# One attention and feed-forward block on one core: q and k as two float32r parts in 64-row tiles, in place of three bf16 parts, and a new order of the work

## The chip, the core and the metric

The kernel runs on one core of a Trainium2 chip. The metric is the device time of one execution in microseconds (us). TensorE (PE) does the matrix products, VectorE (DVE), ScalarE (ACT) and GpSimd (POOL) the elementwise work, and SyncE (SP) issues every DMA.

## The reference, cut to what matters

```python
def stablemax3(logits):                      # in place of a softmax
    logits = logits - max(logits, axis=-1)
    pos = 1.0 + x * (1.0 + 0.5 * x * (1.0 + x / 3.0))
    neg = 1.0 / (1.0 - x * (1.0 - 0.5 * x * (1.0 - x / 3.0)))
    s = where(x >= 0, pos, neg); return s / sum(s)
# x is (8, 512, 128); 16 heads of 8 dimensions
sa, ca, ga, sb, cb, gb = (silu(c) @ wmod)    # ga, gb: sign(g) * max(|g|, 0.25)
h = layernorm(x) * (1 + ca) + sa
q, k, v = h @ w_qkv.T                        # per head (512, 8)
o = stablemax3(q @ k.T * 8 ** -0.5) @ v
x = x + ga * (o @ w_out.T + b_out)
h = layernorm(x) * (1 + cb) + sb
f = relu(s0 * ([h, -h] @ K0)) * 2            # K: +1 or -1; widths 512, 512, 128
x = x + gb * (s2 * (relu(s1 * (f @ K1)) * 2 @ K2))
```

After the maximum is taken off, x is never above 0, so only `neg` counts: one over a cubic. The kernel writes that cubic with its root ROOT = -0.596 split off, and takes 1/|.| with a reciprocal square root of a square.

## The kernel before

Eight batches are worked through one after another, each in 16 steps `n`. A step handles 512x512 logits of one head, twice. First with queries on the partitions (`logits`, L486, PSUM tile SA), from which DVE takes each query's maximum (`maxima`, L749). Four heads (a quad) later the 16 columns of maxima are turned by PE (L496), negated by DVE (L761), split in three bf16 parts by POOL (L941 to L949) and brought by DMA (L1072) into rows 96 to 98 of QH, against rows of ones in KH. Second with keys on the partitions (`scores`, L465, PSUM tile Z, two halves `h`): now the matmul takes the maximum off as it goes. ACT squares a half with a shift (L557, `sq`), DVE makes the cubic from it and Z (L737, `cub`), POOL squares the cubic in place (L890; three heads of 16, letter A in ON_POOL, on ACT instead, L567), ACT takes the reciprocal root (L582, `prob`), and PE multiplies with V and a column of ones (`with_v`, L510, tile OP, four heads in four column tiles of 32).

q and k are needed at more precision than one bf16 has. Each is split in three bf16 parts (POOL, L922 to L932), written to DRAM and read back with each part three times, so that 72 rows of one matmul hold all nine products of parts (PARTS = 3, NROW = 72).

Each engine's instructions stand in one fixed order, written out by hand. Besides its head, a step carries a piece of the work of other batches, called misc: the layernorm, q, k and v of the next batch, the output projection x1 of the last one, and the feed-forward layers l0, l1, y of the one before that (`MISC` gives the step and the place, 0 or 1, of each product, `EVENTS` those of the small work). A step on PE is

```python
logits(n, (0, 1)); with_v(n); scores(b, n + 1, 0); misc_at(pe, b, n, 0)
logits(n, (2,)); maxima_across(n); logits(n, (3,)); misc_at(pe, b, n, 1); scores(b, n + 1, 1)
```

on DVE cubic, maxima, misc, cubic, maxima, misc, and on ACT square, relu, square, prob of two heads back (BEHIND = 2), relu. Waits that tie them: a half of Z is free when DVE has read it (`z_taken`, s_cv); a bank of SA when its maxima are taken (s_mx); one of F_RING = 3 buffers of `cub` when its `prob` is made (s_p); the DMAs of a quad's maxima must have landed before its scores (s_mrow). MB is one PSUM bank for all misc products. The loop is unrolled.

Of the kernel before, what the change touches and what calls it, by code (L numbers as in the profile page):

```python
# [7 lines left out]
BF16 = mybir.dt.bfloat16  # L8
# [18 lines left out]
PARTS = 3  # L27
NROW = PARTS * PARTS * HD
MROW = 96

EPS = 1e-5
TWO_ONES = float(np.array([0x3F803F80], np.uint32).view(np.float32)[0])
E_DMAS = PARTS + 1
SCALE = HD ** -0.5
FIRST = -1

F_RING = 3
P_RING = 8
# [24 lines left out]
def short(name, off, step, place=0, point="e"):  # L69
    return name, off, [(step, place, CHUNKS)], (step, point)  # L70


def long_(name, off, step):

    return name, off, [(step, 0, CHUNKS // 2), (step, 1, CHUNKS // 2)], (step + 1, "s")


MISC = [
    short("hT", 1, 0), short("q", 1, 1), short("k", 1, 2), short("h2T", -2, 3),
    short("l0_0", -2, 4), short("l0_1", -2, 5), short("l0_2", -2, 6), short("l0_3", -2, 7), short("v", 1, 8),  # L80
    long_("l1_0", -2, 9), long_("l1_1", -2, 10), long_("l1_2", -2, 11), short("x1", -1, 12), long_("l1_3", -2, 13),
    ("y", -2, [(14, 0, 2), (14, 1, 1), (15, 0, 1)], (15, "e")),
]
# [11 lines left out]
EVENTS = {
    "den_sq": (7, 1), "den_inv": (8, 0), "att": (8, 1, "pool"), "st2": (13, 0), "mv2": (14, 0), "rs2": (14, 1),  # L100
    "x1n": (15, 0, "pool"), "w2g": (11, 1), "wog": (5, 1), "xbg": (7, 1),
}
# [8 lines left out]
def is_first(b):
    return isinstance(b, int) and b == FIRST


def misc_of(b):
    return MISC_LAST.get(b, MISC) if isinstance(b, int) else MISC


def event(b, name):
    return EVENTS_LAST.get(b, {}).get(name, EVENTS[name]) if isinstance(b, int) else EVENTS[name]  # L120


def live(beta):

    return not isinstance(beta, int) or 0 <= beta < B


def adaln_block(nc, x, w_qkv, w_out, b_out, k0, k1, k2, s0, s1, s2, c, wmod, out):
    x_t = x.rearrange("b (t p) d -> p (b t) d", p=P)

    parts_q = nc.dram_tensor("parts_q", (NQ, PARTS, QUAD * HD, S), BF16, kind="Internal").ap()
    parts_k = nc.dram_tensor("parts_k", (NQ, PARTS, QUAD * HD, S), BF16, kind="Internal").ap()
# [3 lines left out]
    with ExitStack() as ctx:  # L136
# [80 lines left out]
        k2u = k_u8[:, 4096:4096 + KC * D].rearrange("p (a n) -> p a n", a=KC)  # L217

# [5 lines left out]
        s_apart = sem("s_apart")  # L224
# [19 lines left out]
        s_w2g = sem("s_w2g")  # L244
        s_parts = {n: sem("s_parts_" + n) for n in "qk"}
# [4 lines left out]
        s_fa = sem("s_fa")  # L250
# [44 lines left out]
        def apart(eng, b):


            if not isinstance(b, int):
                eng.sem_inc(s_apart)

        def z_taken(eng, b, n, h):

            need(eng, s_cv, 2 * H * b + 2 * n + h + 1)

        def quad_before(b, n):

            return (b, n // QUAD + 1) if n // QUAD < NQ - 1 else (b + 1, 0)


        tail = [(b, i) for b in (B - 1, B, B + 1) for i, m in enumerate(misc_of(b))  # L310
                if b > B - 1 or m[2][0][0] > 8]
# [11 lines left out]
        def products_at(b, n, points):

            return [(name, b + off, bank_of(b, i)[0]) for i, (name, off, _, (step, point)) in enumerate(misc_of(b))
                    if step == n and point in points and live(b + off)]

        def logits_bank(b, beta, h, qt):

            pair = (TB * h + qt) // 2  # L330
            if is_first(b) and pair % 3:
                return Z[:, pair % 3 - 1, :].rearrange("p (t s) -> p t s", t=2)
            return SA

        def batches(body):

            def run(eng):
                for b in range(FIRST, B + 2):
                    body(b)
            return run  # L340
# [775 lines left out]
```

## Time and profile before

| | |
|---|---|
| device time, median of 3 runs | 837.32 us (834.61 to 837.56) |
| profiled execution, its own time | 835.29 us |
| its span, first to last instruction | 833.5 us |
| mean granted clock of TensorE | 0.948 of full speed |
| busy PE / DVE / ACT / POOL | 78% / 80% / 74% / 71% of the span |

1.8 us of the profiled execution lie outside the span. A busy share counts the union of an engine's instructions; four engines between 71% and 80% mean that they work in turns somewhere, and only stretches of the trace tell where.

### The profile page before, as it was taken

What the parts mean: (1) busy time and instruction counts of PE and PEld (TensorE: products, weight loads), DVE (VectorE), ACT (ScalarE), POOL (GpSimd) and SP (SyncE); (2) the same over time, 40 slices, a digit from 0 to 9 for tenths busy, and PEclk for the clock granted to TensorE, in tenths of its full rate; (3) what the DMA queues carried; (4) which work ended last, traced back from release to release, by engine and by line L of the source; (5) the groups of instructions that cost most, each with busy time, mean ns of one, the idle gap of its engine ahead of it and who ended that gap; (6) DMA issues with size and microseconds to landing.
All of it is one profiled execution on the core that took longest, in us unless ns stands there. A gap on an engine that the chain in (4) does not pass through costs nothing.

```text
span 833.5 us, 9550 instructions
## 1 busy us (share of the span) xinstructions
PE 648.3 (78%) x2897; PEld 224.3 (27%) x2897; DVE 664.4 (80%) x785; ACT 620.6 (74%) x541; POOL 595.3 (71%) x507
## 2 busy tenths in 40 slices
PE   3076777777777898779977898679877997996887
PEld 2022111111121333223422342123421342341244
DVE  5389899989997889887998889798997889866120
ACT  1005789889888888698788788698779789889621
POOL 7306887789887967977887967977798677775310
PEclk9968599989999999999999999999999999997999
DMA  2211111210221002210131012210221012000100
GB/s 79 71 60 55 49 38 54 71 56 24 71 65 52 28 28 84 76 41 0 59 94 56 20 39 84 69 37 7 63 80 60 6 42 71 7 8 6 44 22 13
DMA packets 34996, 39.39 MB, mean 47 GB/s; under 512 B 6376, under 2 KB 28160, under 8 KB 34944
## 3 DMA queue, kind: packets, MB, share of 16 engines
q1 hardware_dynamic: 34944, 38.77, 14.7%
q8 instruction: 24, 0.39, 0.2%
q14 instruction: 28, 0.23, 0.1%
HBM read 25.77 MB, written 8.40 MB: 41 GB/s over the span
## 4 chain that ended last, share of the span: by engine, by line
PE 37%; DVE 22%; issue 15%; POOL 14%; ACT 10%; DMA 2%; DVEq 0%; ACTq 0%; SPq 0%; POOLq 0%
PE MB L435 11%; DVE mx L749 10%; DVE cub L737 8%; POOL cub L890 7%; PE Z L465 6%; PE OP L510 5%; PE SA L486 5%; ACT sq L557 4%; ACT prob L582 2%; PE SA L435 2%; POOL rem L925 2%; PE MB L444 2%; PE MB L428 2%; POOL SQ L932 1%; ACT cub L567 1%
## 5 line engine op out<-in xcount | busy, mean ns | idle before, releaser
L890 POOL TENSOR_TENSOR cub<-cub 128x2048 f32<-128x2048 f32 x104 | 373.8, 3597 | 66.5 <-DVE cub L737 66.5
L737 DVE SCALAR_TENSOR_TENSOR cub<-sq,Z 128x1024 f32<-128x1024 f32 x256 | 309.4, 1210 | 48.5 <-ACT sq L557 48.3
L749 DVE TENSOR_REDUCE mx<-SA 128x2 f32<-128x1024 f32 (+1 forms) x277 | 303.1, 1098 | 53.4 <-PE SA L486 51.7
L557 ACT ACTIVATE sq<-Z,shift 128x1024 f32<-128x1024 f32 x256 | 281.3, 1114 | 69.8 <-PE Z L465 68.9
L582 ACT ACTIVATE prob<-cub 128x2048 f32<-128x2048 f32 x128 | 244.7, 1912 | 35.9 <-POOL cub L890 35.9
L486 PE MATMUL SA<-KH,QH 96*128 96x512 bf16 x492 | 165.9, 400 | 89.8 <-DVE mx L749 42.8
L465 PE MATMUL Z<-QH,KH 128*128 128x512 bf16 x512 | 162.5, 400 | 68.0 <-DVE cub L737 66.0
L510 PE MATMUL OP<-prob,Vq 128*16 128x512 f32 x1024 | 140.1, 622 | 3.1 <-ACT OT L612 3.1
L435 PE MATMUL MB<-hid,W 128*128 128x512 f32 x216 | 101.2, 593 | 0.9 <-ACT hid L600 0.9
L486 PEld LDWEIGHTS SA<-KH,QH 96*128 96x128 bf16 x492 | 42.0, 100 | 216.5 <-issue 108.2
L465 PEld LDWEIGHTS Z<-QH,KH 128*128 128x128 bf16 x512 | 35.7, 99 | 234.7 <-DVE cub L737 161.6
L600 ACT ACTIVATE hid<-MB,sv 128x512 f32<-128x512 f32 x54 | 37.0, 686 | 52.3 <-PE MB L435 43.3
L941 POOL TENSOR_SCALAR mp<-ms 16x128 bf16<-16x128 f32 x32 | 9.2, 288 | 80.0 <-DVE ms L761 80.0
L435 PEld LDWEIGHTS MB<-hid,W 128*128 128x128 f32 x216 | 40.6, 189 | 37.6 <-issue 30.7
L567 ACT ACTIVATE cub<-cub 128x2048 f32<-128x2048 f32 x24 | 45.8, 1909 | 0.0
L428 PE MATMUL MB<-h2T,W 128*128 128x512 f32 x54 | 32.9, 696 | 0.0
L510 PEld LDWEIGHTS OP<-prob,Vq 128*16 128x16 f32 x1024 | 17.4, 95 | 56.6 <-issue 53.5
L860 POOL TENSOR_TENSOR rs<-mv,eps 128x4 f32<-128x4 f32 x16 | 3.2, 197 | 31.1 <-DVE mv L790 26.1
L444 PEld LDWEIGHTS MB<-W2G,hid 128*128 128x128 f32 x192 | 23.9, 192 | 2.2
L444 PE MATMUL MB<-W2G,hid 128*128 128x128 f32 x192 | 24.0, 275 | 0.0
L612 ACT ACTIVATE OT<-OP 128x512 f32<-128x512 f32 x32 | 18.9, 591 | 5.4 <-PE OP L510 5.4
L833 DVE TENSOR_TENSOR y<-SA,x1k 128x512 f32<-128x512 f32 x2 | 1.4, 690 | 26.2 <-PE SA L444 26.2
(125 smaller groups left out, 508.6 us busy)
## 6 DMA issues: line engine op xcount, KB each, us to landing
QH<-parts_q SPq DMA_DIRECT2D x96, 96.0 KB
KH<-parts_k SPq DMA_DIRECT2D x32, 288.0 KB
nd<-OT SPq DMA_DIRECT2D x128, 32.0 KB
parts_q<-SQ SPq DMA_DIRECT2D x24, 128.0 KB
parts_k<-SK SPq DMA_DIRECT2D x24, 128.0 KB
xa<-L_attn_x SPq DMA_DIRECT2D x8, 256.0 KB, 8.7
xb<-L_attn_x SPq DMA_DIRECT2D x8, 256.0 KB, 8.9
out<-y SPq DMA_DIRECT2D x8, 256.0 KB, 2.2
```

Of the source, the lines that this page charges most:

```text
L428: mm = nc.tensor.matmul(bank, W0[:, m * P:(m + 1) * P], h2T[:, :], start=True, stop=True)
L435: mm = nc.tensor.matmul(bank, W1[:, kc, m * P:(m + 1) * P], hid[0][:, kc, :], start=(kc == 0), stop=(kc == KC - 1))
L444: mm = nc.tensor.matmul(bank4[:, t, :], hid[1][:, kc, t * P:(t + 1) * P], W2G[:, kc, :], start=(kc == 0), stop=(kc == KC - 1))
L465: mm = nc.tensor.matmul(Z[:, h, t * S:(t + 1) * S], KH[:, n, k0_:k0_ + P], QH[:, n, :], start=True, stop=True)
L486: nc.tensor.matmul(logits_bank(b, beta, hh, qt)[:, qt % 2, :], QH[0:MROW, hh, qt * P:(qt + 1) * P], KH[0:MROW, hh, :], start=True, stop=Tr ...
L510: mm = nc.tensor.matmul(OP[32 * j:32 * j + 2 * HD, :], Vq[:, tb, hh, :, :].rearrange("p d a -> p (d a)"), prob[:, hh % P_RING, tb * S:(tb ...
L557: nc.scalar.activation(sq[:, h, :], Z[:, h, :], ACT.Square, bias=shift[:, 0:1]).then_inc(s_sq, 1)
L567: nc.scalar.activation(f, f, ACT.Square).then_inc(s_fa, 1)
L582: nc.scalar.activation(prob[:, m % P_RING, :], cub[:, (H * beta + m) % F_RING].rearrange("p a n -> p (a n)"), RSQRT).then_inc(s_p, 1)
L737: nc.vector.scalar_tensor_tensor(cub[:, (H * b + n) % F_RING, h, :], sq[:, h, :], CUB_ADD, Z[:, h, :], ALU.add, ALU.mult).then_inc(s_cv, 1)
L749: nc.vector.tensor_reduce(mx[:, g % 2, j * TB + qts[0]:j * TB + qts[-1] + 1], logits_bank(b, beta, QUAD * g + j, qts[0])[:, qts[0] % 2:qts ...
L890: nc.gpsimd.tensor_tensor(ff, ff, ff, ALU.mult).then_inc(s_fp, 1)
```

## The change

q and k are split in two float32r parts (a 4-byte type whose writer rounds away the low bits of the mantissa): the first part is the rounded copy that ACT writes, the second is the rest, made by DVE in one pass. All four products of parts take 32 rows. Row 32 is a product of 0 and 1, rows 33 and 34 hold the two parts of the maximum, 35 and 36 the constant. So scores contract 37 rows and logits 33, and two heads stand beside each other at rows 0 and 64 (`e`), each matmul in a row tile of 64 with an output bank of its own. A step (`m`, `group`) is no longer one head: it is two heads by half of the keys for scores, two heads by two blocks of queries for logits. Each unit of DVE and ACT stays 128x1024.

The maxima are split by DVE (L679, L681) in place of POOL; all 128 squares of the cubic are on POOL; `cub` and `prob` have 4 buffers; `prob` stands one step behind in place of two (BEHIND = 1); the products with V end at the 8th step after the quad's first in place of the 10th; the maxima run 6 steps ahead of the scores (AHEAD = 6). Misc products stand at three places of a step (a, c, d), mostly one matmul each. The large memsets of QH and KH are gone; small constants are written and brought in by DMA.

```diff
-PARTS = 3
+PARTS = 2
-ON_POOL = "PPPPPAPPPPAPPPPA"
-BEHIND = 2
+RING = 4
+AHEAD = 6
+BEHIND = 1
+AV_BEHIND = 4
-    long_("l1_0", -2, 9), long_("l1_1", -2, 10), long_("l1_2", -2, 11), short("x1", -1, 12), long_("l1_3", -2, 13),
+    ("l1_0", -2, [(3, "a", 1), (3, "c", 1), (3, "d", 1), (4, "a", 1)]),
+    ("x1", -1, [(8, "a", 4)]),
...
-        QH = sb("QH", [P, H, S], BF16)
+        QH = sb("QH", [P, 2 * NQ, S], F32R)
...
+                for e in range(2):
+                    rows = slice(64 * e, 64 * e + K_Z)
+                    mm = nc.tensor.matmul(Z[:, h, e * S:(e + 1) * S], KH[rows, 2 * g + r, keys], QH[rows, 2 * g + r, :],
+                                          start=True, stop=True)
+                mm.then_inc(s_z, 1)
...
+            m = s + AHEAD
+            scores(s + 1, 0)
+            if m % QUAD == 0 and m >= QUAD:
+                logits(m, 0, (1,))
+            misc("a")
+            logits(m, 1, (0, 1))
+            with_v(s)
+            scores(s + 1, 1)
+            misc("c")
+            maxima_across(m)
+            logits(m + 1, 0, (0,) if (m + 1) % QUAD == 0 and m + 1 >= QUAD else (0, 1))
+            misc("d")
...
+            square_of(s + 1, 0)
+            take("a")
+            square_of(s + 1, 1)
+            take("c")
+            take_numerators(s)
+            prob_of(s - BEHIND)
+            take("d")
...
-                nc.vector.tensor_scalar(ms[:, :], SA[0:QUAD * TB, 1, 0:P], -1.0, MAX_SHIFT, ALU.mult, ALU.add)\
+                nc.vector.tensor_copy(mp[:, i, 0, :], SA[0:QUAD * TB, 1, 0:P]).then_inc(s_mh, 1)
+                dve.wait_ge(s_mh, quad + 1)
+                nc.vector.tensor_tensor(mp[:, i, 1, :], SA[0:QUAD * TB, 1, 0:P], mp[:, i, 0, :].bitcast(F32), ALU.subtract)\
+                    .then_inc(s_mp, 1)
...
+            cubic(s, 0)
+            take_maxima(m)
+                maxima(m, 0, (0, 1))
+            split(b, n)
+            cubic(s, 1)
+            maxima(m, 1, (0, 1))
+            take(b, n, "a")
+            misc()
...
-            nc.gpsimd.memset(QH[:, :, :].bitcast(F32), 0.0).then_inc(s_one, 1)
-            nc.gpsimd.memset(KH[:, :, :].bitcast(F32), 0.0).then_inc(s_one, 1)
-                        nc.gpsimd.tensor_tensor(dst[:, 2, :], rem[:, i, :], dst[:, 1, :], ALU.subtract)\
...
+            if (s + AHEAD - 4) % QUAD == 0 and 0 <= s + AHEAD - 4 < GROUPS:
+                sp.wait_ge(s_mp, quad + 1)
+                for e in range(2):
+                    for a in range(PARTS):
+                        r = 64 * e + R_MAX + a
+                        sp.dma_start(QH[r:r + 1, 2 * g:2 * g + 2, :].bitcast(F32), mp[2 * TB * e:2 * TB * (e + 1), quad % 2, a, :].bitcast(F32))\
+                            .then_inc(s_mrow[g], 16)
```

What stands on PE where the second layer of the feed-forward (l1, `MB<-hid,W`) runs, before (SA is logits, Z scores, OP the products with V; L435 is l1):

```order
L486 MATMUL SA<-KH,QH 128x512 x2
L510 MATMUL OP<-prob,Vq 16x512 x4
L465 MATMUL Z<-QH,KH 128x512 x2
L435 MATMUL MB<-hid,W 128x512 x2
L486 MATMUL SA<-KH,QH 128x512 x2
L435 MATMUL MB<-hid,W 128x512 x2
L465 MATMUL Z<-QH,KH 128x512 x2
```

and in the changed program (L446 logits, L427 scores, L467 V, L387 l1):

```order
L427 MATMUL Z<-QH,KH 128x512 x2
L387 MATMUL MB<-hid,W 128x512
L446 MATMUL SA<-KH,QH 128x512 x2
L467 MATMUL OP<-prob,Vq 16x512 x4
L427 MATMUL Z<-QH,KH 128x512 x2
L387 MATMUL MB<-hid,W 128x512
L446 MATMUL SA<-KH,QH 128x512 x2
L387 MATMUL MB<-hid,W 128x512
```

Two l1 products in a row stood ahead of logits or scores; now one does, and the scores' first half stands ahead of all else in the step.

On POOL at the split of q and k of the next batch, before (cub is the square of the cubic, SQ and SK the parts of q and k, rem the rest):

```order
L890 TENSOR_TENSOR cub<-cub 128x2048
L922 TENSOR_SCALAR SQ<-rem 128x512
L925 TENSOR_TENSOR rem<-rem,SQ 128x512
L929 TENSOR_SCALAR SQ<-rem 128x512
L932 TENSOR_TENSOR SQ<-rem,SQ 128x512
L890 TENSOR_TENSOR cub<-cub 128x2048
L922 TENSOR_SCALAR SK<-rem 128x512
```

and in the changed program, from the same steps to the two layernorms (L774, L776 roots, L814 xn and x1n):

```order
L808 TENSOR_TENSOR cub<-cub 128x2048 x4
L824 COPY Vq<-Vn 128x4x32
L837 TENSOR_TENSOR woG<-wo,gA 128x128
L808 TENSOR_TENSOR cub<-cub 128x2048
...
L814 TENSOR_SCALAR xn<-xa,mv,rs 128x128 x4
L808 TENSOR_TENSOR cub<-cub 128x2048
L774 TENSOR_TENSOR rs<-mv,eps 128x4
L776 TENSOR_TENSOR rs<-rs,half 128x4
L814 TENSOR_SCALAR x1n<-x,mv,rs 128x128 x4
```

The eight passes on q and k have left POOL; both layernorms now follow each other with one square between them.

On DVE at the maxima of a quad, before (L761 negates them, L749 reduces):

```order
L737 SCALAR_TENSOR_TENSOR cub<-sq,Z 128x1024
L761 TENSOR_SCALAR ms<-SA 16x128
L749 TENSOR_REDUCE mx<-SA 128x1 x2
L737 SCALAR_TENSOR_TENSOR cub<-sq,Z 128x1024
```

and in the changed program (L657 cubic, L679 and L681 the two parts, L690 the second part of k):

```order
L657 SCALAR_TENSOR_TENSOR cub<-sq,Z 128x1024
L679 CAST mp<-SA 16x128
L681 TENSOR_TENSOR mp<-SA,mp 16x128
L668 TENSOR_REDUCE mx<-SA 128x1 x2
L690 SCALAR_TENSOR_TENSOR SK<-MB,SK 128x512
L657 SCALAR_TENSOR_TENSOR cub<-sq,Z 128x1024
```

One small pass of DVE per quad is added, and POOL no longer stands between DVE and the DMA.

## Rows read from the trace of the kernel before

**Rows 1.** The page: the span, and each engine's busy time and instructions

```profile
span 833.5 us, 9550 instructions
PE 648.3 (78%) x2897; PEld 224.3 (27%) x2897; DVE 664.4 (80%) x785; ACT 620.6 (74%) x541; POOL 595.3 (71%) x507
```

**Rows 2.** Windows: stretch, length, busy PE, PEld, DVE, ACT, POOL, clock, DMA

```profile
61.60:150.50 88.90, 64.58 (x256) 15.10 (x256) 83.93 (x91) 70.14 (x57) 65.06 (x49) 0.85 0.17 54
...
239.40:328.20 88.80, 74.10 (x353) 26.87 (x352) 76.76 (x91) 73.41 (x65) 71.75 (x64) 0.98 0.14 44
```

**Rows 3.** The same windows for line L737, the cubic: DVE busy, count

```profile
61.60:150.50 88.90, 41.07 (x34) 0.85 0.17 54
...
239.40:328.20 88.80, 37.52 (x31) 0.98 0.14 44
```

**Rows 4.** Groups by line and shape: busy, mean ns, idle before and its releaser

```profile
L890 POOL TENSOR_TENSOR cub<-cub 128x2048 f32<-128x2048 f32 x104 | 373.8, 3597 | 66.5 <-DVE cub L737 66.5
L737 DVE SCALAR_TENSOR_TENSOR cub<-sq,Z 128x1024 f32<-128x1024 f32 x256 | 309.4, 1210 | 48.5 <-ACT sq L557 48.3
...
L749 DVE TENSOR_REDUCE mx<-SA 128x2 f32<-128x1024 f32 x215 | 262.1, 1219 | 53.0 <-PE SA L486 51.3 <-issue 1.1
...
L435 PE MATMUL MB<-hid,W 128*128 128x512 f32 x216 | 101.2, 593 | 0.9 <-ACT hid L600 0.9
L567 ACT ACTIVATE cub<-cub 128x2048 f32<-128x2048 f32 x24 | 45.8, 1909 | 0.0
...
L761 DVE TENSOR_SCALAR ms<-SA 16x128 f32<-16x128 f32 x32 | 8.8, 274 | 3.0 <-PE SA L496 2.7
```

**Rows 5.** Timeline of DVE in the third batch: start, us, idle before

```profile
338.31 1.21 DVE L749 TENSOR_REDUCE mx<-SA 128x2 f32<-128x1024 f32 x1
339.45 1.21 DVE L737 SCALAR_TENSOR_TENSOR cub<-sq,Z 128x1024 f32<-128x1024 f32 x1
...
343.00 1.22 DVE L737 SCALAR_TENSOR_TENSOR cub<-sq,Z 128x1024 f32<-128x1024 f32 x1 [1.21 <-ACT sq L557]
```

**Rows 6.** Timeline of PE around one product with V

```profile
310.78 0.60 PE L486 MATMUL SA<-KH,QH 96*128 96x512 bf16 x2
...
311.30 1.05 PE L510 MATMUL OP<-prob,Vq 128*16 128x512 f32 x8
...
312.29 0.60 PE L465 MATMUL Z<-QH,KH 128*128 128x512 bf16 x2
...
312.73 1.95 PE L444 MATMUL MB<-W2G,hid 128*128 128x128 f32 x16
```

**Rows 7.** Timeline of POOL: first and last of four passes on q, and on maxima

```profile
239.66 0.62 POOL L922 TENSOR_SCALAR SQ<-rem 128x512 bf16<-128x512 f32 x1 [1.82 <-DVE rem L816]
...
242.31 1.16 POOL L932 TENSOR_TENSOR SQ<-rem,SQ 128x512 bf16<-128x512 f32 x1
...
258.11 0.29 POOL L941 TENSOR_SCALAR mp<-ms 16x128 bf16<-16x128 f32 x1
...
259.36 0.42 POOL L949 TENSOR_TENSOR mp<-mrem,mp 16x128 bf16<-16x128 f32 x1
```

**Rows 8.** Timeline: the first layernorm, first logits, first scores, last cubics, a last layernorm

```profile
6.37 7.17 DVE L681 TENSOR_SCALAR xn<-xa,mv,rs 128x128 f32<-128x128 f32 x4
...
41.41 1.01 PE L486 MATMUL SA<-KH,QH 96*128 96x512 bf16 x2 [19.06 <-DMA KH<-parts_k]
...
61.59 1.01 PE L465 MATMUL Z<-QH,KH 128*128 128x512 bf16 x2 [1.32 <-DVE mx L749]
...
774.30 2.35 DVE L737 SCALAR_TENSOR_TENSOR cub<-sq,Z 128x1024 f32<-128x1024 f32 x2 [3.01 <-ACT sq L557]
...
802.43 1.11 DVE L799 TENSOR_SCALAR x1n<-x,mv,rs 128x128 f32<-128x128 f32 x4 [1.41 <-POOL rs L862]
```

**Rows 9.** Line L1072, the DMAs of the maxima: issue ns, and landing

```profile
L1072 SPq DMA_DIRECT2D QH<-mp x96: 524/585/3390, 56.9 to 742.0; - x96
DMA to landing us min/median/max: 1.7/2.2/7.4
```

More of the change, by code:

```diff
@@ L111, in is_first @@
[L111 to L120, printed above, removed]
-def live(beta):
-    return not isinstance(beta, int) or 0 <= beta < B
+MAIN = [
[10 rows of a table added]
+]
+MISC = {b: MAIN for b in range(FIRST, B - 1)}
+MISC[B - 1] = [
[9 rows of a table added]
+]
+MISC[B] = [
[6 rows of a table added]
+]
+MISC[B + 1] = [
+    ("l1_2", -2, [(0, "a", 2), (0, "c", 2)]), ("l1_3", -2, [(1, "a", 2), (1, "c", 2)]),
+    ("y", -2, [(2, "a", 4)]),
+]
@@ new lines, with group @@
+BY_DVE = ("x1", "v", "y")
+MAIN_AT = {"xbg": 6, "wog": 5, "den_sq": 6, "den_inv": 7, "att": 7, "st2": 9, "mv2": 10, "rs2": 11, "x1n": 11,
+           "w2g": 8, "st1": 6, "mv1": 7, "rs1": 9, "xn": 10}
+AT = {b: MAIN_AT for b in range(FIRST, B)}
+AT[B - 1] = MAIN_AT | {"w2g": 4, "st2": 8, "mv2": 9, "rs2": 9, "x1n": 9}
+AT[B] = MAIN_AT | {"w2g": 2, "st2": 8, "mv2": 8, "rs2": 9, "x1n": 9}
+AT[B + 1] = MAIN_AT | {"w2g": 0}
+TAIL = ("att", "x1n")
+def live(beta):
+    return 0 <= beta < B
+def group(m):
+    i = m % QUAD
+    return m // H, m % H // QUAD, i % 2, i // 2 * 2
@@ L290, in need @@
         def need(eng, s, n):
-            if not isinstance(n, int) or n > 0:
+            if n > 0:
                 eng.wait_ge(s, n)
[L295 to L311, printed above, removed]
@@ L323, in products_at @@
[L323 to L340, printed above, removed]
@@ L345, in adaln_block, with unit_bank, unit_before, steps @@
+        def unit_bank(m, u):
+            k = 2 * m + u
+            return Z[:, k % 3 - 1, :].rearrange("p (e s) -> p e s", e=2) if k < 8 and k % 3 else SA
+        def unit_before(m, u):
+            k = 2 * m + u
+            return 2 * (k - 2) if k < 8 else 2 * k
+        def steps(body):
+            for s in range(FIRST * H, (B + 2) * H):
+                body(s)
+        def at(s, name, beta_off, b, n):
+            return AT[b][name] == n and live(b + beta_off)
         block = ctx.enter_context(nc.Block())
@@ new lines, in logits @@
+                if heads[0] == 0:
+                    if m == 0 and u == 0:
+                        pe.wait_ge(s_gate, 1)
+                        pe.wait_ge(s_rows, 4 * 16)
+                    if m % QUAD == 0 and u == 0:
+                        pe.wait_ge(s_qk[g], (beta + 1) * LOADS * 16)
+                    need(pe, s_mx, unit_before(m, u))
+                else:
+                    need(pe, s_mp, m // QUAD)
+                for e in heads:
+                    rows = slice(64 * e, 64 * e + K_LOG)
+                    nc.tensor.matmul(unit_bank(m, u)[:, e, :], QH[rows, 2 * g + r, qt * P:(qt + 1) * P],
+                                     KH[rows, 2 * g + r, :], start=True, stop=True).then_inc(s_a, 1)
@@ L995, in pool_batch @@
-            for n in range(H):
-                misc(n, 0)
-                square_of(n)
-                misc(n, 1)
+            if n == 0 and live(b - 2):
+                pool.wait_ge(s_taken["x1"], b - 1)
+                need(pool, s_taken["y"], b - 2)
+                nc.gpsimd.tensor_scalar(x1k[:, :, :], x1[:, :, :], 1.0, 0.0, ALU.mult, ALU.add).then_inc(s_x1k, 1)
+            if n in (1, 5):
+                v_in(b, 2 if n == 1 else 3)
+            if n in (13, 14):
+                v_in(b + 1, n - 13)
```

840 lines of the change are left out of this document (340 added, 500 removed), and 23 rows, old and new, of tables (MAIN, MISC).

## The prediction

> **What bounds the kernel now.** I read the page first. Four engines are busy 71% to 80% of 833.5 us [rows 1], so none bounds the whole, and the stretches decide. The windows, cut at 88.9 us from the first scores on, show two regimes. In the first one, before any feed-forward work has begun, DVE is busy 83.93 of 88.90 us, 94%: the kernel runs at DVE's pace. In the third, with l0, l1 and y on PE, DVE is busy 76.76 of 88.80, 86%, and no other engine is fuller [rows 2]. The same windows for the cubic turn that into steps, since each step has two cubics: 34 of them in 88.90 us are 5.23 us a step, 31 in 88.80 are 5.73 [rows 3]. DVE's own work is 76.76 / 15.5 = 4.95 us a step, the rest is waiting. The groups say for what: the cubic waited 48.5 us in all for ACT's squares, the maxima 53.0 for PE's logits, and POOL's squares 66.5 for DVE [rows 4]. Where DVE is fed, a 128x1024 pass starts every 1.14 us (338.31 to 339.45); at 343.00 it stood 1.21 us for ACT [rows 5]. That comes after POOL has spent about 3.8 us on q (239.66 to 243.47) and as much on k between two squares [rows 7]: POOL late, ACT's prob late, ACT's next square late. So the reader is to see a kernel near DVE's limit, with some 12 us of waiting in each of the batches that carry feed-forward work.
>
> **The change, part by part.**
>
> *DVE.* Cubics and maxima stay 512 passes of 128x1024. q and k keep one pass each. Added are one small pass per quad, like the 0.274 us of L761 [rows 4], and a wait of it on the one before, which I put at 0.1: 0.37 x 4 / 16 = 0.09 a step. DVE's work becomes 4.95 + 0.09 = 5.04 us a step.
>
> *POOL.* It loses the passes on q and k, 3.8 us each of which 3.6 are work, 16 times, and on the maxima 1.7 us (258.11 to 259.78), 1.4 of it work, 32 times [rows 7]: 57 + 45. It gains 24 squares. All 128 at 3.597 are 460; the other work was 595.3 - 373.8 = 221.5 [rows 1, 4], less 102, less about 8 of memsets. Sum 571, or 71 us a batch of 16 steps: under DVE's 81, by little. From n = 5 to 11 seven squares (25.2) meet both layernorms, w2g, att, xbg and the roots, which I add up to 14 us: 39 against 37 in which DVE does its seven steps. With four cub buffers a square may be late by roughly a step before ACT is held, so I charge little.
>
> *ACT.* It loses 24 squares of 1.909, 5.7 us a batch [rows 4], and gains two copies of q and k. It has room.
>
> *PE.* Eight matmuls of 512 columns a step, 0.44 for two (312.29 to 312.73) [rows 6], 1.76 in all. The trace has no float32r and no row tile. Bounds for a pair of heads: below, one bf16 matmul, 0.22; above, two l1 products, each two passes of 101.2 / 216 = 0.47 [rows 4], 1.9. I take 0.22 to 0.25. For the single pass speaks that the operand carries fewer bits than the f32 of l1, which pays two recorded passes. For side by side speaks the product with V: four f32 matmuls of 512 columns, in four column tiles, take 0.99 (311.30 to 312.29), where four l1 products one after another take 3.8 [rows 4, 6]. So PE saves about 0.85 a step, 14 us a batch. Against that stand switches between tilings, since every misc product now lies between row tiles. The column-tiled product starts 0.52 after the logits ahead of it where 0.44 would be due [rows 6]; I call it 0.1 a switch, and 29 misc pieces a batch, two switches each, make 6 us. PE: 74.10 a window, 76 a batch, less 14, plus 6 = 68 of 84. The Trainium skill (TensorEngine Tiling (Array Packing), Key Properties) says that a change of tiling mode, not just of tile, drains TensorE; the 0.08 above agrees in kind. By the rule with this price PE has 68, without it 62, and the forecast is 790 by either, as PE is last in neither; only at 0.4 a switch, 23 us, would it be.
>
> *Order.* Say DVE's step begins at 0 with cubic 0. Cubic 0 ends at 1.15, maxima 0 at 2.3, cubic 1 at 3.45, maxima 1 at 4.6. PE makes scores 0 at 1.2, one l1 product until 2.5, logits by 2.9 (due 3.45), V until 4.0, scores 1 by 4.4, one product until 5.4, logits by 5.8 (due 6.2). Each misc place holds one product of 0.94 and fits. Before, two stood together ahead of logits or scores. So I give the batches with feed-forward work the share of DVE that the first had, 95%: 5.04 / 0.95 = 5.3 a step.
>
> *Maxima.* They are made two passes into DVE's step, at 1.85, four DMAs later (3 x 0.585 + 2.2 for the last) they have landed at 5.8; the scores want them at 5.3 + 1.2 = 6.5 [rows 9]. Hidden by 0.7 us. If the landing is 7.4, the longest of before, PE stands 4.5 us, and queued behind it are the logits that DVE needs. At n = 6 SP issues the six loads of the next batch's first quad, which wait for all parts of q and k (1 MB in place of 0.77), ahead of a quad's maxima. I charge 4 us in the run for this and POOL together.
>
> *Start.* The first layernorm took 7.17 us on DVE while POOL wrote QH and KH; the same four passes took 1.11 at 802.43 [rows 8]. That is up to 6 us, I take 5. The parts leave sooner, with more bytes, and I let these cancel but for 1: first logits at 41.4 - 5 + 1 = 37.5. From there to the first scores were 20.2 us. Now four steps' maxima (8 x 1.14), turning and splitting (about 1.5) and the DMA (4) make 15: first scores at 53, against 61.6.
>
> *End.* From the end of the last cubic (774.30 + 2.35 = 776.65) to 833.5 are 56.9 us, nearly all the second half of the last batch's feed-forward work on PE, as before. I take 57.
>
> **The sum.** Before: 61.6 + 715 + 56.9 = 833.5. After: 53, then 112 steps x 5.3 = 594, 80 for the last batch (10 steps at 5.3, 6 without maxima at 4.5, bound by ACT and POOL) and 4 for the waits, then 57: 788, and 1.8 outside the span: 790 against 835.3 profiled. The runs' median is 837.3, 0.25% higher, which I leave within the range.
>
> **The rivals.**
>
> *Row tiles run one after another* (15%). A pair costs 0.44, PE is at 68 + 14 = 82 us a batch, as full as DVE, and logits behind a misc product come 0.3 late. Five batches with feed-forward work at 5.6 a step: 790 + 24 = 814.
>
> *The maxima's DMA or POOL's clump is last* (15%). Once a batch the maxima land 2 to 4 us late, behind loads, or x1n's four passes hold a square by over a step. 8 x 3 = 24: 814.
>
> *DVE is fed throughout* (10%). 98% in place of 95%: 5.14 a step, 18 us less: 771. Against it speaks that even without feed-forward work before had 94%.
>
> *A float32r matmul is no single pass* (9%): the slower side. PE without these matmuls is 68 - 14 = 54 us a batch; with p for a pair, 54 + 64 p. Eight such batches and the 110 us of start and end pass today's 833 at p = 0.57; at p = 0.7 they give 900, and at 0.94, an l1 product's price with the two heads side by side, 1020. I name 900.
>
> *Nothing is gained* (6%): PE, less busy, is granted 1.2 GHz for long. The first window had 0.85 of 2.4 GHz and still 5.23 a step [rows 2, 3]; at half speed all through PE would need 136 us a batch and so be full, which no row shows at that clock; at three quarters on average 68 / 0.75 = 91 a batch, as now: 835. The Trainium skill (TensorE: Matmul & The Clock Gate, HAM oscillation) holds that idle gaps make the clock fall; the 0.98 of the third window agrees as far as it goes, with PE busy there at 74.10.
>
> **How the numbers follow.** The forecast has 45%: 790, its own range 778 to 802. The range reaches down to 768 for DVE fed throughout and up to 822 for the two rivals at 814; outside are the last two and the tails of the others, 2 in 10. A measurement of this kernel can tell about 0.5% from no change. Faster: 45 + 10 + 15 + 15 = 85%. Within 0.5%: 4 of the last rival's 6. Slower: 9 + 2 = 11%.
>
> **What would show it.** Windows of the loop: 5.3 us a step in batches with and without feed-forward work, DVE at 95%. A pair's logits and scores start within 0.05 us of each other, and the next matmul 0.22 after. First scores at 53, xn under 3 us. PE waits for `QH<-mp` under 5 us in all, cubic for ACT under 20. No idle of ACT on POOL's squares beyond a few us, near n = 11. The forecast is wrong if pairs start 0.22 apart or more, if the maxima's DMAs stand in PE's waits with over 20 us, or if the clock in the middle windows is below 0.9 with PE on the chain.

## The result: 892.7 us against 836.7, the kernel is 6.7% slower

The changed kernel takes 892.7 us (median of 4 runs, 890.68 to 894.96) against 836.7 for the one before (834.61 to 837.56): a ratio of 1.067, 95% interval 1.064 to 1.071. The forecast was 790, its range 768 to 822.

The page of the changed kernel, profiled at a mean granted clock of 0.843 where before had 0.948:

```profile
span 888.7 us, 9519 instructions
PE 743.6 (84%) x2897; PEld 263.7 (30%) x2897; DVE 667.8 (75%) x814; ACT 591.1 (67%) x531; POOL 580.6 (65%) x350
```

As many matmuls as before take 743.6 us of PE in place of 648.3 [rows 1], where some 60 us fewer were forecast. DVE, POOL and ACT have the work that was worked out for them (POOL 571 forecast). The same 88.9 us windows as [rows 2, 3], the first from the first scores on, for all engines and then for the cubic, now L657:

```profile
58.40:147.30 88.90, 70.75 (x238) 23.65 (x238) 78.08 (x86) 60.70 (x51) 59.29 (x25) 0.97 0.13 43
239.40:328.20 88.80, 79.71 (x339) 28.34 (x337) 75.29 (x89) 68.35 (x62) 67.94 (x40) 0.88 0.16 49
...
58.40:147.30 88.90, 37.56 (x31) 0.97 0.13 43
239.40:328.20 88.80, 35.08 (x29) 0.88 0.16 49
```

31 and 29 cubics: 5.74 and 6.12 us a step, where before had 5.23 and 5.73 and the forecast 5.3. DVE is busy 88% and 85% of them, PE 90% of the second. The groups, in the columns of [rows 4]:

```profile
L668 DVE TENSOR_REDUCE mx<-SA 128x2 f32<-128x1024 f32 (+1 forms) x282 | 311.5, 1105 | 119.9 <-PE SA L446 117.3
L657 DVE SCALAR_TENSOR_TENSOR cub<-sq,Z 128x1024 f32<-128x1024 f32 x256 | 309.6, 1210 | 16.8 <-ACT sq L507 16.8
L518 ACT ACTIVATE prob<-cub 128x2048 f32<-128x2048 f32 x128 | 243.8, 1905 | 2.4 <-POOL cub L808 2.4
...
L387 PE MATMUL MB<-hid,W 128*128 128x512 f32 x216 | 128.2, 683 | 0.6 <-ACT hid L544 0.6
```

DVE's waits for ACT fell from 48.3 to 16.8 us and ACT waits 2.4 for POOL, as the change means it. The waits of the maxima for PE's logits rose from 51.7 to 117.3. And l1, whose matmuls the change doesn't touch, has a mean of 683 ns for 593 [rows 4].

Two views show why PE is late. First the clock. Windows of 600 us from the middle of the loop, first of the kernel before and then of the changed one, columns as in [rows 2]:

```profile
150.00:750.00 600.00, 493.99 (x2317) 171.32 (x2315) 523.10 (x598) 504.25 (x438) 481.49 (x407) 0.98 0.15 48
```

```profile
150.00:750.00 600.00, 538.07 (x2152) 183.56 (x2148) 500.41 (x585) 450.05 (x403) 439.49 (x252) 0.81 0.15 47
```

PE is busier and yet granted 0.81 in place of 0.98. The four f32 matmuls with V (one for each head of a quad, two recorded passes each) show it piece by piece: of the 128 such groups, 120 ran in 0.98 us and 5 at half speed (1.84) before, with 3 between; after, 70 and 44, with 14 between.

Second, what a step costs at full speed, by the lengths of its matmuls. The timeline of PE (y is L396, scores L427, logits L446, V L467; the last row is the first half of a piece), and a row of DVE in the same stretch:

```profile
411.02 1.16 PE L396 MATMUL MB<-W2G,hid 128*128 128x128 f32 x8
412.11 0.51 PE L446 MATMUL SA<-KH,QH 33*128 33x512 f32 x2
412.54 1.16 PE L396 MATMUL MB<-W2G,hid 128*128 128x128 f32 x8
413.63 0.50 PE L427 MATMUL Z<-QH,KH 37*128 37x512 f32 x2
414.06 1.16 PE L396 MATMUL MB<-W2G,hid 128*128 128x128 f32 x8
415.15 0.49 PE L446 MATMUL SA<-KH,QH 33*128 33x512 f32 x2
415.57 1.05 PE L467 MATMUL OP<-prob,Vq 128*16 128x512 f32 x8
416.56 0.50 PE L427 MATMUL Z<-QH,KH 37*128 37x512 f32 x2
416.99 0.71 PE L396 MATMUL MB<-W2G,hid 128*128 128x128 f32 x4
```

```profile
415.78 1.23 DVE L668 TENSOR_REDUCE mx<-SA 128x2 f32<-128x1024 f32 x1 [0.68 <-PE SA L446]
```

From start to next start PE has no gap: a misc piece 1.09, a pair 0.43, V 0.99. From 411.02 to 416.99 is one step, 5.97 us of PE alone against 5.04 of DVE's work: DVE stands 0.68 for logits. A pair was costed at 0.22 to 0.25, a misc piece at 0.94. Where no piece of another tiling follows, a pair takes 0.34.

The start and the end, in the same columns:

```profile
6.50 1.52 DVE L598 TENSOR_SCALAR xn<-xa,mv,rs 128x128 f32<-128x128 f32 x4
...
37.49 0.79 PE L446 MATMUL SA<-KH,QH 33*128 33x512 f32 x2 [20.66 <-DMA KH<-parts_k]
...
58.38 0.79 PE L427 MATMUL Z<-QH,KH 37*128 37x512 f32 x2 [4.11 <-DMA QH<-mp]
...
820.92 2.35 DVE L657 SCALAR_TENSOR_TENSOR cub<-sq,Z 128x1024 f32<-128x1024 f32 x2 [2.48 <-ACT sq L507]
```

So the span is 58.4, a loop of 764.9 to the end of the last cubic (823.3), and 65.4 behind it, against the forecast's 53, 678 and 57. In the chain of waits, PE has 59% of the span and the DMA of the maxima 4%.

### The profile page after: what moved, and what is told of

Its sections match the earlier page's. It is cut to its first block, busy times and chain, and to the rows that moved or that the text cites. A ratio compares the mean times of both kernels' runs of the same rounds, so it can differ in the third digit from the quotient of the medians.

```text
span 888.7 us, 9519 instructions
## 1 busy us (share of the span) xinstructions
PE 743.6 (84%) x2897; PEld 263.7 (30%) x2897; DVE 667.8 (75%) x814; ACT 591.1 (67%) x531; POOL 580.6 (65%) x350
## 4 chain that ended last, share of the span: by engine, by line
PE 59%; DVE 17%; issue 10%; DMA 6%; ACT 5%; SPq 2%; POOL 1%; DVEq 0%; ACTq 0%; POOLq 0%
PE MB L387 13%; PE OP L467 12%; PE SA L446 10%; PE Z L427 8%; DVE mx L668 7%; DVE cub L657 6%; DMA QH<-mp 4%; PE MB L396 3%; PE MB L380 3%; PE MB L361 3%; PE SA L387 2%; ACT prob L518 2%; SPq L948 2%; ACT sq L507 1%; DMA KH<-parts_k 1%
## 5 line engine op out<-in xcount | busy, mean ns | idle before, releaser
L808 POOL TENSOR_TENSOR cub<-cub 128x2048 f32<-128x2048 f32 x128 | 460.4, 3601 | 185.0 <-DVE cub L657 185.0
L668 DVE TENSOR_REDUCE mx<-SA 128x2 f32<-128x1024 f32 (+1 forms) x282 | 311.5, 1105 | 119.9 <-PE SA L446 117.3
L657 DVE SCALAR_TENSOR_TENSOR cub<-sq,Z 128x1024 f32<-128x1024 f32 x256 | 309.6, 1210 | 16.8 <-ACT sq L507 16.8
L446 PE MATMUL SA<-KH,QH 33*128 33x512 f32 x502 | 169.6, 600 | 64.9 <-DVE mx L668 44.1
L427 PE MATMUL Z<-QH,KH 37*128 37x512 f32 x512 | 157.4, 585 | 42.5 <-DVE cub L657 28.5
L467 PE MATMUL OP<-prob,Vq 128*16 128x512 f32 x1024 | 178.9, 780 | 0.0
L427 PEld LDWEIGHTS Z<-QH,KH 37*128 37x128 f32 x512 | 60.3, 223 | 237.3 <-issue 118.6
L387 PE MATMUL MB<-hid,W 128*128 128x512 f32 x216 | 128.2, 683 | 0.6 <-ACT hid L544 0.6
L446 PEld LDWEIGHTS SA<-KH,QH 33*128 33x128 f32 x502 | 64.8, 228 | 210.5 <-issue 103.1
L387 PEld LDWEIGHTS MB<-hid,W 128*128 128x128 f32 x216 | 34.3, 196 | 31.8 <-issue 29.6
L396 PE MATMUL MB<-W2G,hid 128*128 128x128 f32 x224 | 31.9, 287 | 0.9 <-ACT hid L544 0.9
L467 PEld LDWEIGHTS OP<-prob,Vq 128*16 128x16 f32 x1024 | 17.5, 99 | 46.2 <-issue 40.7
L774 POOL TENSOR_TENSOR rs<-mv,eps 128x4 f32<-128x4 f32 x16 | 3.3, 204 | 40.7 <-DVE mv L736 27.7
L396 PEld LDWEIGHTS MB<-W2G,hid 128*128 128x128 f32 x224 | 27.0, 191 | 8.4 <-issue 8.4
L824 POOL COPY Vq<-Vn 128x128 f32<-128x128 f32 x32 | 9.6, 301 | 25.0 <-DVE Vn L708 25.0
L814 POOL TENSOR_SCALAR x1n<-x,mv,rs 128x128 f32<-128x128 f32 x28 | 21.9, 794 | 0.7
L814 POOL TENSOR_SCALAR xn<-xa,mv,rs 128x128 f32<-128x128 f32 x28 | 21.9, 794 | 0.1
```

Source lines behind the costliest of these rows:

```text
L387: mm = nc.tensor.matmul(bank, W1[:, kc, m * P:(m + 1) * P], hid[0][:, kc, :], start=(kc == 0), stop=(kc == KC - 1))
L396: mm = nc.tensor.matmul(bank4[:, t, :], hid[1][:, kc, t * P:(t + 1) * P], W2G[:, kc, :], start=(kc == 0), stop=(kc == KC - 1))
L427: mm = nc.tensor.matmul(Z[:, h, e * S:(e + 1) * S], KH[rows, 2 * g + r, keys], QH[rows, 2 * g + r, :], start=True, stop=True)
L446: nc.tensor.matmul(unit_bank(m, u)[:, e, :], QH[rows, 2 * g + r, qt * P:(qt + 1) * P], KH[rows, 2 * g + r, :], start=True, stop=True).then ...
L467: mm = nc.tensor.matmul(OP[32 * j:32 * j + 2 * HD, :], Vq[:, tb, hh, :, :].rearrange("p d a -> p (d a)"), slot[:, tb % 2, j % 2, :], start ...
L657: nc.vector.scalar_tensor_tensor(cub[:, m % RING, h, :], sq[:, h, :], CUB_ADD, Z[:, h, :], ALU.add, ALU.mult).then_inc(s_cv, 1)
```

## The experiments

"From first to last cubic" below is the start of the first to the end of the last: 711.9 us before, 762.4 after. Ratios are to the kernel before, run on the same chip.

**What the tiles, the type and the rows cost.** Four kernels, each the changed one with other operands for scores and logits. `x_f32r_whole` contracts all 128 rows of both heads, so it has no row tiles; its sums mix two heads. `x_bf16_tiles` reads the upper half of each word as bf16, so that its products are less precise. `x_bf16_whole` does both. `x_f32r_rows64` keeps the tiles, and contracts all 64 rows of each, the added ones zeros (in logits also the rows of old maxima). Those with added rows write QH and KH full of zeros first.

```diff
-                    rows = slice(64 * e, 64 * e + K_Z)
+                    rows = slice(0, P)                # whole; rows64: slice(64 * e, 64 * e + 64)
...
-                    KH[rows, 2 * g + r, keys], QH[rows, 2 * g + r, :]
+                    KH[rows, 2 * g + r, keys].bitcast(BF16)[:, 1::2], QH[...].bitcast(BF16)[:, 1::2]   # bf16
...
+            nc.gpsimd.memset(QH[:, :, :].bitcast(F32), 0.0).then_inc(s_fill, 1)     # whole, rows64
+            nc.gpsimd.memset(KH[:, :, :].bitcast(F32), 0.0).then_inc(s_fill, 1)
```

> The changed kernel (892.7 us) with scores and logits contracted over all 128 rows, both heads' rows at once, still float32r; the logits and scores are wrong sums, and QH and KH are filled with zeros at the start. No row tiles are left, so no switch between row tiles and whole matmuls. Theory A (in the changed kernel the two row tiles do not save time over two whole matmuls, and the switches and the low clock that go with them are what it lost): a pair still holds PE 0.43 us, a misc product falls from about 1.0 back to 0.86, and V runs at full speed (1.05 us) in most steps; 845 to 865 us. Theory B (the tiles do work side by side, but one float32r matmul takes 0.43 us): a pair now holds 0.86, 4 x 0.43 us more in each step, 990 us or more. Theory C (the order of the work is what lost): within 1% of 892.

> The changed kernel with scores and logits reading the upper halves of the same float32r words as bf16, in the same row tiles; less precise q, k and maxima. Theory A: a pair still holds 0.43 us, 885 to 895 us, the clock as low. Theory B: a pair falls to 0.22, four pairs a step, 845 to 865 us. Theory C: within 1% of 892.

> Both edits: bf16 halves, contracted over all 128 rows, no row tiles; wrong sums. This is the matmul of the kernel before in the order of the changed one. Theory A: pair 0.43 us, clock as in the kernel before (0.95), 840 to 860 us; not far from x_f32r_whole. Theory B: the same time here, but 130 us under x_f32r_whole. Theory C: within 1% of 892.

> The changed kernel with both tiles contracting all their 64 rows (those above 37 are zero; logits now also contract stale rows of the maxima, so they are wrong). Time of a matmul and switches are the same. If the clock fell because few rows work, V runs at half speed in fewer of its 128 products and the time falls to 860 to 880 us; if rows don't matter, 892 within 1%.

Measured, with the clock of the profiled run. The last column is a step with three l1 products in which PE has no gap, from V to V at full speed:

| | time, us | ratio (95%) | clock | first to last cubic | first cubic at | step with three l1 |
|---|---|---|---|---|---|---|
| after | 892.7 | 1.067 (1.064 to 1.071) | 0.843 | 762.4 | 60.9 | 5.85 |
| x_f32r_rows64 | 865.35 | 1.034 (1.024 to 1.045) | 0.884 | 729.7 | 69.2 | 5.85 |
| x_bf16_tiles | 860.88 | 1.029 (1.018 to 1.040) | 0.849 | 731.1 | 60.6 | 5.48 |
| x_f32r_whole | 852.82 | 1.019 (1.009 to 1.030) | 0.957 | 716.1 | 70.1 | 5.60 |
| x_bf16_whole | 850.32 | 1.016 (1.005 to 1.028) | 0.930 | 714.7 | 69.7 | 5.47 |

The fill costs the kernels that have it some 9 us before the first cubic, so rows64 is 33 us faster than after where both do the same. It differs from after in the rows contracted and the fill alone: PE works on 27 and 31 more rows, nearly all zeros, each matmul takes as long as before (0.50 us recorded), and the clock rises. Its products with V are at full speed 98 times and at half 20, against 70 and 44. So the number of rows at work moves the clock, and giving the rows back returns 33 of the 50 us that the loop lost.

That is not yet a share of the loss. x_bf16_tiles has as few rows as after and a clock as low (46 products with V at half speed, 73 at full), and it gets 31 of the 50 us back as well, by its shorter steps. The rows with their clock, and the type, are each worth some 30 us while the other is as it is. All these kernels also work on other numbers than after; no run changes the numbers alone.

What a switch of tiling costs stands in the timelines, y at full speed between two pairs, of x_bf16_tiles and of x_f32r_whole:

```profile
404.33 0.40 PE L428 MATMUL Z<-QH,KH 37*128 37x512 bf16 x2
404.66 1.16 PE L397 MATMUL MB<-W2G,hid 128*128 128x128 f32 x8
405.75 0.40 PE L447 MATMUL SA<-KH,QH 33*128 33x512 bf16 x2
405.99 0.39 PE L428 MATMUL Z<-QH,KH 37*128 37x512 bf16 x2
```

```profile
403.63 0.73 PE L428 MATMUL Z<-QH,KH 128*128 128x512 f32 x2
404.20 1.05 PE L397 MATMUL MB<-W2G,hid 128*128 128x128 f32 x8
405.01 0.71 PE L447 MATMUL SA<-KH,QH 128*128 128x512 f32 x2
```

Two tiles do run side by side: with logits and scores behind each other, a bf16 pair takes 0.24 (405.75 to 405.99), as forecast, and 0.33 ahead of another tiling. With float32r it is 0.34 and 0.43. Its weight load is longer too, 0.18 for 0.095 us each; that this is the reason is likely, and no run shows it. Where the records part a pair from the piece behind it differs from kernel to kernel, so take the two together. From one l1 product over a pair to the next are 1.48 us in float32r tiles, 1.39 in bf16 tiles, 1.32 and 1.31 on the whole array; a pair and y have 1.52, 1.42, 1.38 and 1.36. So next to a piece the tiles cost some 0.15 us in float32r and 0.07 in bf16. Between two pairs they save 0.2 instead. By the last column, tiles in bf16 cost PE nothing in such a step and in float32r 0.25 us, and float32r costs 0.37 more than bf16 in tiles, 0.13 on the whole array. A float32r matmul is a single pass in every tiling.

**The maxima's DMA.** The waits for it that the trace gives PE and PE's weight loads add up to 33 us in after. Most of these stretches are in both lists; PE itself stood 13.1 us, 4.11 of them ahead of the first scores. Making the maxima a step earlier takes the waits off PE, if the rest stays.

```diff
-AHEAD = 6
+AHEAD = 7
```

> The changed kernel with the maxima, the loads of q and k and the DMAs of the maxima one step earlier (AHEAD 7 in place of 6), nothing else. PE waited 33 us for the DMAs of the maxima in the changed kernel. Theory D (these DMAs are on the path): the wait falls under 8 us and the time by 10 to 25 us, to 868 to 883. Theory A (they only fill time that PE's other delays make): the wait goes, the time stays within 5 us of 892.

> x_f32r_whole (852.8 us, wrong sums, no row tiles) with AHEAD 7. There PE waited some 50 us for the DMAs of the maxima. Theory D: 825 to 838 us, at or below the kernel before. Otherwise within 5 us of 852.

That the time falls was wrong in both. `x_ahead7`: 899.28 us, 1.076 (1.070 to 1.083), at the edge of what after has; PE stood 8.7 us in place of 13.1. `x_whole_ahead7`: 862.92, 1.034 (1.031 to 1.038), 10 us slower than x_f32r_whole; PE stood 29.6 us in place of 33.5. So neither run took the wait away, and neither shows what it costs. x_f32r_whole at one quad, from the timeline of SP, the chain of waits and the timeline of PE:

```profile
393.50 2.70 SPq L952 DMA_DIRECT2D QH<-mp  x4
...
395.57 5.00 DMA QH<-mp
...
400.62 0.74 PE L428 MATMUL Z<-QH,KH 128*128 128x512 f32 x2 [1.09 <-DMA QH<-mp]
```

and x_whole_ahead7 in the same place:

```profile
398.54 1.19 SPq L939 DMA_DIRECT2D KH<-parts_k  x2
399.84 2.70 SPq L952 DMA_DIRECT2D QH<-mp  x4
...
401.92 7.63 DMA QH<-mp
...
409.59 0.74 PE L428 MATMUL Z<-QH,KH 128*128 128x512 f32 x2 [0.99 <-DMA QH<-mp]
```

With AHEAD 7 SP issues the four DMAs directly behind the six loads of the next quad's q and k, 0.1 us after them in most quads, where with AHEAD 6 it was 2 us or more. From the issue of the last one to PE's scores they then take 7.2 to 9.1 us (the 20 times that they stand in the chain), against 3.0 to 6.9 with AHEAD 6. What the step gained was lost on the way; that the loads in front are the reason is not shown. Where no tiles slow PE down, the DMA is on the path: it has 11% of the chain of waits in x_f32r_whole and 12% in x_bf16_whole, where PE stands 41.1 us for it, against 4% in after; in the kernel before PE never waits for it.

**The rows alone.** The kernel before with fewer rows in its matmuls, nothing else changed. Both leave the maxima out of the scores; `b_rows37` also leaves out part of the products of q and k.

```diff
-    KH[:, n, k0_:k0_ + P], QH[:, n, :]
+    KH[0:72, n, k0_:k0_ + P], QH[0:72, n, :]          # b_rows37: 0:37
...
-    QH[0:MROW, hh, qt * P:(qt + 1) * P], KH[0:MROW, hh, :]
+    QH[0:72, hh, qt * P:(qt + 1) * P], KH[0:72, hh, :]
```

> The kernel before with scores and logits contracting the first 72 rows alone (no maximum is taken off in the scores, so the output is wrong); still whole-array bf16 matmuls, same durations and order. If the number of rows at work sets the clock, V runs at half speed in more than the 5 to 10 of 128 products of before, and the time rises by 5 to 25 us; if not, 835 within 1%.

> The same with 37 rows: few rows as in one tile of the changed kernel, and a row tile of 64, so with switches, but without two heads side by side; wrong output. By rows and switches: half speed in over 40 of 128 products with V, l1 products next to scores hold PE 0.2 us longer, 880 to 920 us. If neither rows nor switches cost, 835 within 1%.

`b_rows72`: 859.44 us, 1.030 (1.021 to 1.038), clock 0.861. 72 rows in place of 128 and 96, with instructions, order, DMAs and tiling as they were, cost 25 us. (The numbers behind the scores change with it, since no maximum is taken off.) The middle windows of the loop:

```profile
150.00:750.00 600.00, 506.74 (x2217) 166.53 (x2216) 513.97 (x582) 490.33 (x423) 465.11 (x392) 0.91 0.16 49
```

Pairs and V have their old lengths at full speed, but 26 of the 128 products with V are at half speed, for 5. `b_rows37`: 1038.6 us in the profiled run, far above the 880 to 920 expected, span 1036.8, clock 0.659. Its timeline at 400 us (L409 is q):

```profile
400.52 1.91 PE L510 MATMUL OP<-prob,Vq 128*16 128x512 f32 x8
402.36 1.03 PE L465 MATMUL Z<-QH,KH 37*128 37x512 bf16 x2
403.32 2.07 PE L409 MATMUL MB<-hT,wq 128*128 128x512 f32 x2
405.32 1.03 PE L486 MATMUL SA<-KH,QH 37*128 37x512 bf16 x2
```

V takes 1.84 us where [rows 6] has 0.99, two matmuls 0.96 for 0.44. PE is busy 94% of the middle windows, and still 78 of its 128 products with V are at half speed, 42 at full. This run has switches of tiling as well as fewer rows, so it doesn't part the two; b_rows72 and x_f32r_rows64 do.

**Fewer switches.** If the switches cost what they seem to, products of l1 and y in pairs should save half of them.

```diff
-    ("l1_0", -2, [(3, "a", 1), (3, "c", 1), (3, "d", 1), (4, "a", 1)]),
+    ("l1_0", -2, [(3, "a", 2), (3, "c", 2)]),
...
-    ("y", -2, [(10, "c", 1), (10, "d", 1), (11, "a", 1), (11, "c", 1)]),
+    ("y", -2, [(10, "c", 2), (11, "a", 2)]),
```

> The changed kernel with l1 and y in pairs: two products at one place of a step in place of one at each of two places (a and c of every second step and so on), in the seven main batches. The row tiles, the element work and the DMAs are the same, the number of l1 and y pieces between tiles is halved, 20 to 10 a batch. Theory (each piece between row tiles costs PE 0.2 to 0.3 us): PE gains 2 to 3 us a batch in the six batches with feed-forward work, 12 to 18 us in all: 875 to 880, if the clock stays as it is. Rival (the order by single products feeds DVE better, and the switches are hidden): each pair of products of 1.9 us now stands ahead of logits or scores, DVE waits up to 1 us more there, and the time is 895 to 905.

937.93 us, 1.124 (1.120 to 1.128), clock 0.728. My theory lost, and the rival had too little: 45 us slower than after. The saving is there, two l1 products in 1.91 in place of 2 x 1.05, and it is swamped. DVE in the fourth batch, behind y's first two products (3.5 us on PE, most of it at half speed):

```profile
430.75 1.23 DVE L668 TENSOR_REDUCE mx<-SA 128x2 f32<-128x1024 f32 x1 [2.44 <-PE SA L446]
```

The maxima's waits for logits are 159.3 us in all, for 117.3. So in this kernel products one by one, the change's order, feed DVE better than pairs, and what stands ahead of the logits counts for more than PE's sum. The clock is lower too, with 55 products with V at half speed for 44, and the run doesn't part the two.

**The start.** What the change does to the first layernorm, by itself, on the kernel before: the zero fill of KH stands until xn is made.

```diff
             root_of(0, mv1, rs1, s_ve1, s_rs1)
+            pool.wait_ge(s_xn, 1)
             nc.gpsimd.memset(KH[:, :, :].bitcast(F32), 0.0).then_inc(s_one, 1)
```

> The kernel before with one wait added: POOL's zero fill of KH stands until DVE has made the first xn. Theory (the fill beside it is what stretches xn to 7.17 us): xn falls to about 1.5 us, the first logits and scores come some 5 us sooner (36.5 and 56.5), nothing behind them changes: about 830 against 835, ratio 0.994. Rival (the start hangs on the loads of weights or on POOL's later fills, which now come 1.5 us later): the first scores stay within 1 us of 61.6 and the time at 835.

829.11 us, ratio 0.9945 (0.9924 to 0.9966), the fastest version here:

```profile
6.50 1.12 DVE L681 TENSOR_SCALAR xn<-xa,mv,rs 128x128 f32<-128x128 f32 x4
...
37.40 1.01 PE L486 MATMUL SA<-KH,QH 96*128 96x512 bf16 x2 [20.98 <-DMA KH<-parts_k]
...
57.97 0.63 PE L465 MATMUL Z<-QH,KH 128*128 128x512 bf16 x1 [1.70 <-DVE mx L749]
```

xn takes 1.12 us for 7.17, the first logits come 4.0 sooner, the first scores 3.6 [rows 8], where 5 was expected. The Trainium skill (SBUF — State Buffer, SBUF: two separate sides) says that GpSimd and VectorE, in those of its modes that use both its port pairs, share one pair of ports, held by one for a whole instruction while the other is blocked; these rows agree, with 7.17 beside the fill and 1.12 without.

## Why the prediction was wrong, point by point

Three steps of it failed: every price was taken at the full clock, PE's work was put too low, and the gain given to the new order, 37 us, isn't there.

**The clock: the rival "Nothing is gained", 6%.** The forecast let every price stand at the full clock, and put the clock into one rival with "PE, less busy, is granted 1.2 GHz for long", at 835. The clock did fall, and not because PE was less busy: it was busier. What fell is the number of rows at work in a matmul, 128 and 96 to two tiles of 37 and 33. b_rows72 shows that on the old kernel with nothing else in its program changed (+25 us), rows64 on the new one (-33 in the loop). Nothing in the trace of before could give this price, since its scores, logits and products with V all work on 96 or 128 rows; but that the rows changed was in the diff, and I asked only how long and how often PE works. One of the forecast's own signs of being wrong came true: 0.81 in the middle window, under its 0.9, with PE at 59% of the chain. The Trainium skill (TensorE: Matmul & The Clock Gate, What's actually happening) describes a monitor that goes by how busy PE has been; here PE 84% and 90% busy in the middle windows (b_rows72, after) was granted less than at 82% (before), so busy time alone doesn't order these runs, though part of the higher share comes from the low clock itself.

**PE's price.** "I take 0.22 to 0.25" for a pair: the single pass and the two heads side by side were right, a bf16 pair takes 0.24. Off were the size for float32r, 0.34, and the switches, called "0.1 a switch". A pair and an l1 product together are 0.23 + 0.86 + 0.2 = 1.29 by the forecast, and take 1.48; any other pair takes at least 0.1 more than forecast. With 29 pieces and 35 other pairs a batch, 68 us become 68 + 29 x 0.19 + 35 x 0.1 = 77, at the full clock. The Trainium skill's drain on a change of tiling mode (TensorEngine Tiling (Array Packing), Key Properties) was cited and judged harmless until 0.4 a switch, by the batch's sum. That was the wrong sum: "each misc place holds one product of 0.94 and fits" left some 1.1 us for it, and a step with three pieces is 5.97 us of PE, over DVE's 5.04. Steps with pieces are PE's, those without DVE's, and a mean over a batch shows neither. x_bf16_tiles against x_bf16_whole prices the tiles, clock and switches together, at 731.1 - 714.7 = 16.4 us; at full speed their steps with three l1 products are equal, 5.48 and 5.47, which points at the clock (46 and 11 products with V at half speed).

**The order: "5.04 / 0.95 = 5.3 a step".** Without tiles, in bf16 and near the full clock (x_bf16_whole, 0.98 in the middle of the loop), the new order takes 714.7 us from first to last cubic against 711.9. At 357 to 368 us DVE waits in each step again for logits, since PE is without a gap there:

```profile
357.50:367.50 10.00, 10.00 (x44) 3.83 (x44) 8.60 (x8) 8.85 (x8) 7.20 (x5) 1.00 0.31 104
```

With three pieces of 0.86, four pairs and V a step takes PE 5.5 us with no tiles at all. So the gain of 37 us that the forecast gave to the order isn't there: what was saved in waits for ACT and POOL came back as waits for PE. Within the loop DVE's waits for logits went from 38.7 us to 67.7. PE's full steps are one part of that. The maxima's DMA is the other: its line in the page of x_bf16_whole leads the chain of waits,

```profile
DMA QH<-mp 12%; DVE cub L659 9%; DVE mx L670 8%; PE MB L389 7%; PE Z L429 6%; PE OP L469 6%; SPq L953 5%; PE SA L448 5%; POOL cub L812 3%; ACT prob L520 3%; PE SA L389 2%; ACT sq L509 2%; PE MB L382 2%; PE MB L363 1%; PE MB L398 1%
```

and 18 of DVE's waits for logits, 26.9 us together, end within 3.3 us of such a wait of PE. No run has the new order with the DMA off the path, so what the order is worth by itself stays open. x_grouped shows that single products are no worse than pairs; the other parts of the order (BEHIND, AV_BEHIND, the three places) weren't tried one by one.

**The maxima's DMA** ("under 5 us in all", rival at 15%): PE stood 13.1 us for it in after and 41.1 in x_bf16_whole, so the step that hid it by 0.7 us was wrong. The issue was costed nearly right (2.70 for four, 0.67 each for 0.585), the landing was not: 2.2 by the median of before, where the last DMA's issue to PE's scores took 4.0 to 6.6 us in after when it stood in the chain. In after it is a small cause, since PE is late anyway: 9.0 us of PE's waits in the loop, 5.3 of DVE's behind them. It grows as PE gets faster, and by the chain of waits is one reason that the kernels without tiles end no lower than before.

**Start.** First logits 37.49, forecast 37.5; xn 1.52, and b_start shows the mechanism alone. First scores 58.4 for 53: PE stood 4.11 us for the first maxima, whose four DMAs SP issued in a row over 2.74 us from 49.65, behind the loads of KH. I gave turning, splitting and DMA 5.5 in all.

**End.** 65.4 for "I take 57". The last products with V stand between products of l1 and y and end at 842.3, 19.0 us behind the last cubic, where before ended them at 790.4, 13.8 behind. Nothing is left on PE to cover what hangs on them:

```profile
841.36 1.05 PE L467 MATMUL OP<-prob,Vq 128*16 128x512 f32 x8
842.34 2.05 PE L396 MATMUL MB<-W2G,hid 128*128 128x128 f32 x16
849.72 2.05 PE L369 MATMUL SA<-woG,nd 128*128 128x128 f32 x8 [5.34 <-issue]
```

**Right** were the work of DVE and POOL, DVE's waits for ACT (under 20, 16.8), ACT's for POOL (2.4), and that a pair starts together. **The sum of it:** from 833.5 the span went -3.2 at the start, +49.9 in the loop (764.9 - 715), +8.5 at the end, to 888.7. Of the loop's 50, 33 go when the tiles are filled with rows (762.4 to 729.7), 14 more when the tilings go (to 716.1), and 1 more with float32r (to 714.7), where before had 711.9. In another order the shares differ: float32r in tiles is worth 31 (762.4 to 731.1). They don't add up, since each makes PE faster and leaves the next to wait on DVE or on the maxima's DMA.

## What to carry to other kernels

Before matmuls are packed into fewer rows, ask what the clock will do: here fewer busy rows cost more than the packing gave, and a run of the old kernel on fewer rows tells it beforehand. A switch of tiling has a price, so hold it against the place that the piece has to fit, step by step, and not against a batch's sum. When waits on one releaser are taken away from an engine at 86%, work out what the next ones would let through: here they were PE and the maxima's DMA, at nearly the same pace. And a run that is to take a wait away proves nothing until its trace shows the wait gone.

## What was not expected of the hardware

- Rows at work and the clock: the kernel before with 128 and 96, with 72 and with 37 rows had 5, 26 and 78 of its 128 products with V at half speed, at a mean granted clock of 0.948, 0.861 and 0.659, in 834, 859 and 1039 us; the last also switches tilings.
- The granted clock of the records can disagree with the durations. In the changed kernel the first batches stand at 1.00, and the matmuls in them take what they take at half speed:

```profile
83.00:105.00 22.00, 18.48 (x67) 5.10 (x65) 20.85 (x29) 15.67 (x12) 15.69 (x6) 1.00 0.12 45
```

```profile
91.91 1.91 PE L467 MATMUL OP<-prob,Vq 128*16 128x512 f32 x8
93.75 0.79 PE L427 MATMUL Z<-QH,KH 37*128 37x512 f32 x2
```

  So 0.843 is too high a mean for it (b_rows37's second run took 1056 us at a recorded 0.802, longer than 1039 at 0.659), and of two kernels' clocks the lengths of a matmul that both have are the better witness.
- float32r is a single pass in row tiles and on the whole array alike. In tiles a pair takes 0.1 us more than in bf16; on the whole array a pair and an l1 product together take 1.32 against 1.31.
